# Spreading a batch's 32 row scatters over 24 steps instead of 20 in an attention and mixture-of-experts kernel

## The reference, cut to what matters

```python
x = L0_attn_x                                  # 16 x 512 x 256
x = _layernorm(x + attention(x))               # 16 heads, rope, causal softmax
x = _layernorm(x + experts(x))                 # 32 experts, 8 chosen per token
...
logits = x @ gate_w.T
top_w, top_idx = jax.lax.top_k(softmax(logits), 8)
out += (u * silu(g) @ dw.T) * w_e              # summed over the chosen experts
```

## Time and profile before

| | |
|---|---|
| time, median of 3 runs | 2184.89 us (2176.04 to 2189.03) |
| the profiled execution | 2174.78 us, its span 2173.0 us |
| TensorE matmul busy | 1808.8 us (83%) |
| VectorE busy | 1595.2 us (73%) |
| ScalarE busy | 1356.9 us (62%) |
| GpSimd busy | 1242.9 us (57%) |
| mean granted TensorE clock | 0.946 of 2.4 GHz |
| moved by DMA | 495.04 MB, mean 228 GB/s |

### The profile page before, as it was taken

The page is one execution under the profiler, slowest core; times in us unless marked ns, Lnnn a source line. Parts: engine busy times, 40 slices in busy tenths (PEclk is TensorE's granted clock), DMA queues, the critical chain, the costliest instruction groups (busy, mean ns, idle before and its releaser), DMA issues.

```text
span 2173.0 us, 53996 instructions
## 1 busy us (share of the span) xinstructions
PE 1808.8 (83%) x17104; PEld 1287.2 (59%) x17104; DVE 1595.2 (73%) x3572; ACT 1356.9 (62%) x3265; POOL 1242.9 (57%) x1206
## 2 busy tenths in 40 slices
PE   4999898889888888889878997998888789988920
PEld 3555555555544544555445887897777678777820
DVE  3878878888878888887864545565457678778888
ACT  1556665666564555565445876887767678788820
POOL 1003455444643664546634777777777777778860
PEclk8999999999998999999988999999999999999965
DMA  4455667666755865566667765655689899889977
GB/s 137 114 159 173 210 224 227 192 206 213 237 173 170 283 215 190 181 202 212 207 191 255 245 194 188 215 186 196 214 289 307 298 301 324 293 279 369 349 241 249
DMA packets 242891, 495.04 MB, mean 228 GB/s; under 512 B 47800, under 2 KB 140415, under 8 KB 232848
## 3 DMA queue, kind: packets, MB, share of 16 engines
q1 hardware_dynamic: 158720, 299.30, 44.5%
q0 software_dynamic: 58368, 163.70, 20.5%
q10 hardware_dynamic: 25536, 28.58, 3.9%
HBM read 284.54 MB, written 234.04 MB: 239 GB/s over the span
## 4 chain that ended last, share of the span: by engine, by line
PE 42%; DVE 21%; DMA 12%; issue 10%; POOL 8%; ACT 5%; SPq 2%; ACTq 1%; POOLq 0%; DVEq 0%
DVE mn L1664 6%; POOL y_tokens L904 5%; PE ps L1026 5%; DMA ynum<-attention 4%; PE ps L1145 3%; DMA y_tokens<-work,yidx 3%; PE ps L1146 3%; PE ps L1165 3%; PE ps L1147 3%; PE ps L1051 3%; PE ps L1077 3%; PE ps L1091 3%; PE ps L1104 2%; POOL x_sorted L886 2%; PE ps L1037 2%
## 5 line engine op out<-in xcount | busy, mean ns | idle before, releaser
L1301 ACT ACTIVATE pT<-ps 128x512 f32<-128x512 f32 (+2 forms) x1008 | 666.7, 701 | 312.2 <-PE ps L1079 250.4
L886 POOL DMA_INDIRECT x_sorted<-xhl,idx x512 | 530.3, 1036 | 474.5 <-DVE xhl L1739 232.7
L1664 DVE TENSOR_REDUCE mn<-ps 128x1 f32<-128x512 f32 (+3 forms) x704 | 412.4, 632 | 57.9 <-PE ps L1053 55.5
L1145 PE MATMUL ps<-pT,gu_hi 128*128 128x256 f16 (+1 forms) x1600 | 373.1, 251 | 53.9 <-ACT pT L1301 53.2
L1146 PE MATMUL ps<-pT,gu_hi 128*128 128x256 f16 (+1 forms) x1600 | 372.1, 251 | 0.0
L1147 PE MATMUL ps<-pT,gu_lo 128*128 128x256 f16 (+1 forms) x1600 | 371.6, 251 | 0.0
L1051 PE MATMUL ps<-stacks 96*128 96x512 bf16 (+3 forms) x1024 | 274.6, 310 | 81.6 <-DVE mn L1664 41.2
L904 POOL DMA_INDIRECT y_tokens<-work,yidx x264 | 277.5, 1051 | 79.8 <-issue 58.6
L1077 PE MATMUL ps<-stacks 99*128 99x512 bf16 (+3 forms) x1024 | 283.1, 306 | 22.8 <-ACT pT L1301 18.4
L1079 PE MATMUL ps<-maskk,identb 128*128 128x128 bf16 x1024 | 222.5, 222 | 0.0
L1145 PEld LDWEIGHTS ps<-pT,gu_hi 128*128 x1600 | 158.6, 99 | 80.9 <-issue 67.8
(11 more groups left out here) (255 smaller groups left out, 3842.9 us busy)
## 6 DMA issues: line engine op xcount, KB each, us to landing
stacks<-y_tokens SPq DMA_DIRECT2D x64, 1024.0 KB
stacks<-qk_parts SPq DMA_DIRECT2D x128, 192.0 KB
qk_parts<-pbuf SPq DMA_DIRECT2D x31, 768.0 KB, 4.1
stacks<-qk_parts SPq DMA_DIRECT2D x128, 128.0 KB
attention<-yev ACTq DMA_DIRECT2D x64, 256.0 KB
stacks<-x_sorted SPq DMA_DIRECT2D x52, 304.0 KB, 3.8
x_sorted<-pads_h SPq DMA_DIRECT2D x99, 152.0 KB
pbuf<-x_sorted SPq DMA_DIRECT2D x40, 304.0 KB
```

The costliest lines, as they stand in the source:

```text
L886: pool.indirect_dma_start(xsort[g][:, :], bass.IndirectOffsetOnAxis(ap=at, axis=0), xhl_rows[:, t, :], None).then_inc(s_scat, 16)
L1145: mmul(o, w_hi[k], x_hi[k], start=k == 0, stop=False)
L1301: return nc.scalar.activation(o, i, f, **k)
L1664: V.tensor_reduce(mn[:, tt, h0:h0 + nh], ps[:, odd_bank("max", at, m), 0:nh * n].rearrange("p (a n) -> p a n", a=nh), axis=AX.X, op=ALU.ma ...
```

## The change

One constant is changed. Scatter `j` stands at step `floor(j * SCATTER_STEPS / 32)`, so with 20 the scatters stand at steps 0 to 19, and with 24 at steps 0 to 23.

```diff
--- before.py
+++ after.py
@@ -75,7 +75,7 @@
 SLOT_RANK_IN = 28
 SLOT_EXP = 28
 SLOT_RESIDUAL = 0
-SCATTER_STEPS = 20
+SCATTER_STEPS = 24
 SLOT_WEIGHTS = 31
 SLOT_TABLE = 14
 SLOT_TABLE_OUT = 25
```

## The result

The changed kernel takes 2192.21 us (median of 18 runs, 2179.18 to 2204.32), the kernel before 2181.43 us beside it (18 runs, 2175.72 to 2191.65). The ratio is 1.005 with a 95% interval of 1.0034 to 1.0066, in us 10.8 by the medians. So the change costs time: the interval leaves out 1. The forecast was 2185, with a range of 2166 to 2207; its sum said 0.1 us more than before.

The account below looks back on a forecast made before the run. It took the chain to be TensorE 42%, VectorE 21% and GpSimd 8%, with the root behind the scatters. 1.4 us gained less 1.5 lost left the median at 2185 us, range 2166 to 2207.

Parts of the forecast that it names:

- its sum: Whole run: 1.4 us gained at the root, 1.5 us lost at the cast, 0.1 us more, no change.
- The mechanism ahead of the root: GpSimd works in order: the root stands behind 32 scatters while VectorE waits, 19.0 us in iterations 2 to 15.
- Four pass the root, not five: At GpSimd's root: scatters 28 to 31 move behind it, 28 and 29 ahead of the x1 store.
- The root's saving: VectorE's wait ahead of the mean column: 5.7 us gained, 4.3 us lost over the iterations, net 1.4 us.
- The cover of the tail: ScalarE's cast wait, 9.8 us uncovered, is hidden by slack before VectorE's weights; 1.5 us left in iterations 9 to 13.
- the size of the landing: Scatter 31, issued behind the store: 3.33 us from issue to the cast it releases, through at store + 5.77.
- The slow rival: Scatters 30 and 31 move only after the store lands, holding the cast: 19 us slower, 2204; chance 0.22.
- its sign of 3 us of wait or more: ScalarE's wait ahead of the upper-rows cast: 3 us or more would mean the slow rival holds.

Follow-up runs that it names:

- the control: The kernel before (20 steps) with only ScalarE's upper-rows cast moved from step 26 to step 28: 2180.81 us, ratio 0.9991.

## Why the prediction came out as it did

**The mechanism ahead of the root was right.** The root stands behind the scatters, and what it waits there is VectorE's. With the root ahead of them, 15.6 us of wait went and about 15 us of time.

**Four pass the root, not five**, and 28 and 29 fit in ahead of the store: the store follows the root by 833.53 - 829.62 = 3.91 us, and 3.9 was said.

**The root's saving was right to 0.2 us.** The sum left 19.0 - 1.4 = 17.6 us of idle time (said as 17 to 18); 17.4 were measured. Iteration 10 was to wait 1.6 us and waits 1.67 (3.02 in the earlier trace rows). Iterations 9, 13 and 15 were to lose 1.1, 1.3 and 1.3 us, and their wait grew by 1.06, 1.29 and 1.28 (by the timelines of both, 0.61 to 1.67, 1.32 to 2.61, 2.10 to 3.38). Spreading gives the root little because the scatters kept ahead of it move to later steps too.

**The cover of the tail was right for the gate weights and only partly for the down weights.** The prediction let 0.47 us of each wait be covered in the iterations with gate weights and 1.0 us in those with down weights. Put on the measured waits, that gives (0.55 + 1.18 + 1.92 + 1.64 + 2.04) - 5 x 0.47 = 5.0 us in iterations 3 to 7. VectorE's wait there grew by 0.08, 0.73, 1.46, 1.18 and 1.57 us, each within 0.02 us of it; iteration 2 adds 0.3. In 9 to 13 it gives (4.35 + 2.20 + 1.94 + 2.11 + 1.91) - 5 x 1.0 = 7.5 us, and 5.5 were measured: 3.06, 0.91, 0.66 and 0.82 in iterations 9 to 12, where the cover was 1.3 us, and none in 13. There the prediction counted a cast of down weights behind the upper-rows cast, and none is there: the last one starts at 977.0 us before and 998.3 after, ahead of that iteration's upper-rows cast (1026.9 and 1051.7).

**The step that failed is the size of the landing.** "What a scatter takes from issue to the cast that it releases is seen once: 1400.91 to 1404.24, 3.33 us", and so number 31 was to be through at store + 5.77. That row comes from the second phase, from a quiet stretch. Between the end of the scatter's instruction and the cast (1401.88 to 1404.24) the DMA queues moved this (packets, MB, share of the 16 DMA engines' time):

```profile
q0 software_dynamic: 111, 0.30, 32.3%
q1 hardware_dynamic: 7, 0.01, 2.0%
```

The prediction's remark that the queue "was busy with other transfers as well" in that row holds for GpSimd's own queue q0 at most; the other queues had 2% there, and 20.9% in iteration 10 after (836.94 to 840.30). In the twelve iterations the scatter took 3.35 to 6.48 us, in the median 4.19 and in the mean 4.36, and the last scatter was through at store + 5.78 to + 8.92, in the mean + 6.8. The 1.03 us more in the mean are 12.3 us in 12 iterations. ScalarE came to the cast 0.1 to 0.3 us later than said, 1.5 us in sum, and 9.8 + 12.3 - 1.5 = 20.6 us; 20.5 were measured. For iterations 9 to 13 the prediction had 1.3 us of wait each; 1.91 to 4.35 came.

With the measured waits the prediction's own sum is 5.0 + 7.5 - 1.6 = 10.9 us slower, and the medians say 10.8. That the two agree to 0.1 us is luck: 2.0 of the 7.5 us did not come, and the interval goes from 7.4 to 14.4 us. What VectorE's rows show is 5.3 + 5.5 - 1.6 = 9.2 us.

Iteration 9 is the extreme. Its rows after:

```profile
763.62 0.97 POOL L886 DMA_INDIRECT x_sorted<-xhl,idx  x1 [0.30 <-issue]
...
770.10 1.06 ACT L1301 ACTIVATE xhl<-x 128x1024 f16<-128x1024 f32 x1 [4.35 <-DMA x_sorted<-xhl,idx]
...
772.47 0.69 DVE L1621 TENSOR_TENSOR dn<-work,dn 128x512 f16<-128x512 f32 x1 [3.06 <-ACT dn L1301]
```

6.48 us from issue to cast, and 3.06 of the 5.5 us that VectorE lost to the down weights.

By the fit of the Trainium skill (DMA: Bandwidth & Descriptors, Anatomy of one DMA — SWDGE (gpsimd) path) 2.4 us is the estimate for such a transfer. None of the twelve comes near it; the shortest time that a wait of the cast shows in any kernel does, 2.55 us (24 steps, root at 17, cast at 28, iteration 15).

**The slow rival's place was right and its mechanism holds in part.** It put the cost at the cast held by numbers 30 and 31, at store + 7.4, because they would move only when the store is done. Measured is + 6.8 in the mean, between this and the forecast's + 5.77, and just past the + 6.7 from which it was to decide; its sign of 3 us of wait or more came in iteration 9 alone. The prediction had no row for the order within a queue; the DMA packets have it. The first packets of number 30 start 0.5 to 2.3 us before the store's last one ends, so they do not wait for the whole store. But the last packet of number 31 ends 0.75 to 2.2 us behind the store's last in all 14 iterations, in nine of them 0.75 to 0.78. From its issue it ends after 2.54 us before the change (mean of the twelve), 3.74 after, and 3.24 with the store behind. So some 0.5 of the 1.2 us that it grew by go with the store ahead, and 0.7 do not. The other executions with 24 steps bear this out: 3.51 to 3.76 us with the store ahead (cast at 25, 27 and 28), 3.25 with it behind (cast at 28). The store's landing itself is longer than in the earlier trace rows; the view of L876 after:

```profile
DMA to landing us min/median/max: 3.6/5.4/7.5
```

**Checked against all kernels.** Three waits of VectorE (the mean column in iterations 2 to 15, the gate weights, the down weights), each less its value before and added up, give a time without any other knowledge. This was worked out after the runs.

| kernel | sum of the three, us | ratio from it | measured |
|---|---|---|---|
| the change | -1.6 + 5.3 + 5.5 = 9.2 | 1.0042 | 1.0049 |
| cast at 28 | -1.8 | 0.9992 | 0.9985 |
| cast at 27 | -1.6 | 0.9993 | 0.9986 |
| 20 steps, cast at 28 | -3.6 | 0.9983 | 0.9991 |
| root at 17 | -15.6 + 3.1 = -12.5 | 0.9943 | 0.9932 |
| root at 17, cast at 28 | -15.5 | 0.9929 | 0.9926 |
| 24 steps, root at 17, cast at 28 | -15.5 | 0.9929 | 0.9907 |
| store at 23 | -1.7 + 0.3 + 0.9 = -0.5 | 0.9998 | 1.0032 |
| store at 23, cast at 28 | -1.6 | 0.9993 | 1.0021 |
| only 30 and 31 late | -15.6 + 4.3 + 4.0 = -7.3 | 0.9967 | 1.0013 |
| cast at 25 | -1.6 + 24.7 + 9.0 = 32.1 | 1.0147 | 1.0196 |

The first seven lie inside their intervals. The last four come out 6 to 11 us slower than these waits say. In two of them the store is later; for the other two no cause was found. The granted clock of TensorE, for which the last section has the numbers, was lower in all four than in the kernel before, and is a rival that no run sets apart; it was lower in the change too, which fits without it. The -3.6 us of the control, in which nothing ahead of the root was changed, says how far such a sum moves from one execution to another. What is shown is that the change's cost hangs on the cast's wait: one edit to the cast takes both away with 24 steps and does nothing with 20, and a longer wait costs more. That the cost comes to the end by VectorE's two waits alone is argued from the sum.

## What to carry to other kernels

When instructions are moved from ahead of one waiting engine to later steps, look for the instruction that must wait for the last of them to land: here the gain of 1.6 us at the root was paid for with 20.5 us of wait at the cast, of which about 11 reached the end. A wait counts by what it hands on: in another kernel 13.2 us at the same cast cost nothing. A price taken from one row needs the spread of its neighbours, from the stretch that the change touches, before it may decide a sum: 3.33 us against 3.35 to 6.48 was the difference between no change and 0.5%. And where an urgent small instruction stands behind a long run of others, moving it alone (root at step 17, 0.7% faster) did what spreading the run did not.

## What the runs showed of the hardware that was not expected

The time from a scatter's issue to the instruction it releases is no constant. In the changed kernel it runs from 3.35 us (iteration 15) to 6.48 (iteration 9); with the root at step 17 its median over five iterations is 6.40, with 24 steps besides and the cast at 28 it is 3.30 over eight. A 512 KB store ahead on the same queue explains a part of it, some 0.5 us. Much of the rest goes with what the other queues move meanwhile. The table has five scatters and the shares of the 16 DMA engines' time between the end of the scatter's instruction and the start of the cast:

| last scatter | issue to cast, us | GpSimd's queue q0 | all other queues |
|---|---|---|---|
| 24 steps, root at 17, cast at 28, iteration 11 | 3.12 | 24.6% | 1.7% |
| before, the row | 3.33 | 32.3% | 2.0% |
| the change, iteration 10 | 4.33 | 35.2% | 20.9% |
| the change, iteration 9 | 6.48 | 33.8% | 38.8% |
| 20 steps, root at 17, iteration 11 | 7.12 | 33.7% | 41.1% |

The queues in iteration 9 of the change (764.59 to 770.10: packets, MB, share):

```profile
q0 software_dynamic: 214, 0.73, 33.8%
q1 hardware_dynamic: 134, 0.54, 25.3%
q10 hardware_dynamic: 144, 0.26, 12.7%
q14 instruction: 2, 0.02, 0.8%
```

This is an association and not an experiment: no run moved those transfers, and a scatter that lands later has more time to meet them. Nor does it explain every row: with the cast at 25, iteration 7 has 4.58 us with 0.3% on the other queues (619.50 to 623.11).

The granted clock of TensorE goes with the cost too. Medians over all runs, as a share of 2.4 GHz:

| kernel | granted clock |
|---|---|
| the kernel before, beside the others | 0.944 to 0.945 |
| the change | 0.939 |
| cast at 25 | 0.933 |
| store at 23; only 30 and 31 late; store at 23 and cast at 28 | 0.9405; 0.941; 0.942 |
| cast at 27; cast at 28; 20 steps and cast at 28 | 0.9435 each |
| the three with the root at 17 | 0.9455 to 0.9475 |

In the profiled executions the same 17104 matmuls kept TensorE busy for 1808.8 us before and 1829.0 after. Moving the cast brings the time back, and with it the clock. So the clock is no rival for where the cost comes from; whether it carries a part of it to the end or only follows from the longer waits, these runs do not separate.
